# Second attention: the causal triangles move from TensorE to VectorE

## What is computed

```
q, k, v = to_heads(q), to_heads(k), to_heads(v)        # 16 heads of 16 channels
attn = jnp.einsum('bhqd,bhkd->bhqk', q, k) / math.sqrt(HEAD_DIM)
attn = attn + alibi_bias(seq_len, N_HEADS)[None] + causal_mask(seq_len)[None, None]
attn = jax.nn.softmax(attn, axis=-1)
y = jnp.einsum('bhqk,bhkd->bhqd', attn, v)
```

## Time and profile before

| | us |
|---|---|
| median of 3 runs (2758.51 to 2764.95) | 2764.04 |
| the profiled execution | 2757.35 |
| its span | 2755.6 |
| TensorE busy in the span | 2581.0 |
| VectorE busy | 1872.7 |
| ScalarE busy | 1269.7 |

### The profile page before, as it was taken

How to read it: one execution, slowest core, us unless ns; L and a number is a source line. 1 busy time by engine, 2 the same in 40 slices (tenths; PEclk the granted TensorE clock), 3 DMA queues, 4 the chain that set the end, 5 groups by cost and what they waited for, 6 DMA issues and landing times. The chain is left out here.

```text
span 2755.6 us, 38804 instructions
## 1 busy us (share of the span) xinstructions
PE 2581.0 (94%) x14106; PEld 1255.9 (46%) x14106; DVE 1872.7 (68%) x4022; ACT 1269.7 (46%) x1936; POOL 788.3 (29%) x760
## 2 busy tenths in 40 slices
PE   5987999999999999897999998899999999899998
PEld 3543333333333332354565665445544554555665
DVE  7868888788787885585664335787777776466334
ACT  4431666566566667543212322365454556321321
POOL 2545214132141300155424541311121110234441
PEclk8997999999999999899999999999999999999999
DMA  4004430331303400001303654634223440311565
GB/s 126 1 17 92 64 52 19 58 56 21 58 24 53 64 1 2 1 1 55 109 20 101 158 119 114 118 50 71 48 54 57 65 59 2 115 35 35 139 156 161
DMA packets 162592, 175.76 MB, mean 64 GB/s; under 512 B 19090, under 2 KB 135762, under 8 KB 162258
## 3 DMA queue, kind: packets, MB, share of 16 engines
q1 hardware_dynamic: 146948, 152.57, 25.4%
q0 software_dynamic: 12416, 17.84, 3.9%
q10 hardware_dynamic: 3040, 2.88, 0.4%
HBM read 116.32 MB, written 56.13 MB: 63 GB/s over the span
## 5 line engine op out<-in xcount | busy, mean ns | idle before, releaser
L1862 DVE TENSOR_REDUCE a_mx<-a_bank 128x1 f32<-128x512 f32 (+3 forms) x1792 | 1034.6, 626 | 241.7 <-PE a_bank L1595 173.1
L1730 ACT ACTIVATE a_E<-a_bank 128x1024 f32<-128x1024 f32 (+3 forms) x896 | 796.2, 931 | 401.5 <-PE a_bank L1653 273.7
L1595 PE MATMUL a_bank<-a_KT,a_QT 96*128 96x512 bf16 (+4 forms) x1792 | 572.3, 368 | 25.6 <-DVE a_mx L1862 15.2
L1653 PE MATMUL a_bank<-a_QT,a_KT 99*128 99x512 bf16 (+4 forms) x1792 | 505.1, 357 | 3.9 <-DMA a_QT<-a_mT 1.8
L1668 PE MATMUL a_bank<-a_E,a_Vg 128*32 128x512 f32 (+3 forms) x3584 | 437.3, 560 | 0.7 <-ACT a_E L1730 0.7
L1595 PEld LDWEIGHTS a_bank<-a_KT,a_QT 96*128 96x128 bf16 (+1 forms) x1792 | 152.0, 98 | 490.1 <-DVE a_mx L1862 307.5
L1653 PEld LDWEIGHTS a_bank<-a_QT,a_KT 99*128 99x128 bf16 (+1 forms) x1792 | 169.6, 98 | 173.5 <-ACT a_E L1730 31.4
L435 POOL TENSOR_TENSOR f_hl<-f_hT,f_hh 128x512 f16<-128x512 f32 x96 | 110.9, 1156 | 340.3 <-ACT f_hh L452 340.3
L903 PE MATMUL d_bank<-wdT,d_hT 128*128 128x256 f32 (+1 forms) x768 | 192.4, 393 | 4.2 <-DVE d_hT L1100 4.2
L1014 ACT ACTIVATE d_silu<-d_bank 128x512 f32<-128x512 f32 x96 | 57.1, 595 | 270.0 <-PE d_bank L888 270.0
L903 PEld LDWEIGHTS d_bank<-wdT,d_hT 128*128 128x128 f32 (+1 forms) x768 | 140.2, 191 | 63.2 <-issue 43.6
(11 more groups left out here) (235 smaller groups left out, 3633.9 us busy)
## 6 DMA issues: line engine op xcount, KB each, us to landing
parts<-a_parts SPq DMA_DIRECT2D x64, 384.0 KB, 2.6
a_QT<-parts SPq DMA_DIRECT2D x180, 128.0 KB, 5.9
a_KT<-parts SPq DMA_DIRECT2D x180, 128.0 KB, 9.1
d_wgu<-in_L_ffn_w_gate SPq DMA_DIRECT2D x64, 176.0 KB
d_wgu<-in_L_ffn_w_up SPq DMA_DIRECT2D x64, 176.0 KB
d_wd<-in_L_ffn_w_down SPq DMA_DIRECT2D x64, 176.0 KB
normalised<-d_xn SPq DMA_DIRECT2D x8, 1152.0 KB, 4.7
acc<-d_zero SPq DMA_DIRECT2D x2, 4224.0 KB, 16.4
```

The lines of the kernel that those rows point to most:

```text
L1595: last = nc.tensor.matmul(out[:, 0:w], QT[0:W, h, qt * P:(qt + 1) * P], KT[0:W, h, kh * HALF:kh * HALF + w], start=True, stop=not diag)
L1653: last = nc.tensor.matmul(out, KT[:, h, kt * P:(kt + 1) * P], QT[:, h, half * HALF + c0:(half + 1) * HALF], start=True, stop=not diag)
L1730: nc.scalar.activation(E[:, u % 2, 2 * pair:2 * pair + 2, c0:HALF], bank[:, 2 * pair:2 * pair + 2, c0:HALF], ACT.Exp).then_inc(exps, 1)
L1862: nc.vector.tensor_reduce(mx[:, x[1] // C % 2, j, qt, kh:kh + 1], out[:, 0:w], AX.X, ALU.max).then_inc(freed_dve, 1)
```

## The change

Both triangles leave TensorE. In the first pass VectorE takes the maximum of a diagonal chunk with `tensor_tensor_reduce`, which adds the tile `causal` (zeros, and the triangle in its last 128 columns) to the scores, writes the sum back and gives the maximum. In the second pass a new function `seal` has VectorE add the triangle `later` in place to the first 128 columns of both heads of a pair, one `tensor_tensor` per pair; ScalarE waits for it on a new semaphore `sealed`. The statistics tile `bnr` moves into `yT`. The core of the diff:

```diff
--- before.py
+++ after.py
@@ -40,6 +40,7 @@
 ZERO_POINT = 128.0
 LN_EPS, RMS_EPS = 1e-5, 1e-6
 NEG = -1e30
+LOWEST = -3.0e38
 VW = 32
 ROPE = HD // 2
 LIFT = 1024.0
@@ -1305,6 +1306,7 @@
     units = [(h, kt, max(0, kt - KPH * h) * P if second else 0)
              for h in range(QH) for kt in range(KPH * (h + 1) if second else TPB)]
     U = len(units)
+    diagonal = [u for u in range(U) if second and units[u][1] >= KPH * units[u][0]]
 
     chunks = [(j, qt, kh, min(HALF, (qt + 1) * P - kh * HALF) if second else HALF)
               for h in range(QH) for j in range(GH) for qt in range(h * KPH, (h + 1) * KPH) for kh in range(2)
@@ -1406,8 +1408,9 @@
         bn8 = sb(tag + "bn8", [P, TPB, 6])
         known = TPB if second else NT
         if second:
-            masks = sb(tag + "masks", [P, 2, P], BF16)
-            bnr = sb(tag + "bnr", [P, NT - TPB, 6])
+            causal = sb(tag + "causal", [P, HALF], BF16)
+            later = sb(tag + "later", [P, P], BF16)
+            bnr = yT.rearrange("p a k c -> p (a k c)")[:, 0:(NT - TPB) * 6].rearrange("p (t s) -> p t s", s=6)
         else:
             turns = sb(tag + "turns", [P, 2, T])
         bank = ps(tag + "bank", [P, 8, HALF])
@@ -1417,7 +1420,7 @@
         (root, scales, ones, normed, filled, freed_dve, freed_act, high, rest, mid, split_s, parted, parted_dve, rows_in, v_group, m_step, m_rows, scored, exps, pv, y_kept, y_step, stats,
          aggregated) = (sem(tag + n) for n in names.split())
         if second:
-            masked = sem(tag + "masked")
+            masked, sealed = sem(tag + "masked"), sem(tag + "sealed")
         else:
             t_in, shuffled, roped, roped_dve = (sem(tag + n) for n in ("t_in", "shuffled", "roped", "roped_dve"))
         if second:
@@ -1586,16 +1589,12 @@
                         b, h = G // NG, G % NG * GH + j
                         if x[1] == 0 and second:
                             pe.wait_ge(rows_in, START + 32)
-                            pe.wait_ge(masked, START + 1)
                         if x[1] % C == 0:
                             pe.wait_ge(loaded[G % NG], START + ((b + 1) * 12 + (6 if G % NG == 0 else 0)) * 16)
                         if G == 0 and qt == KPH and j == kh == 0:
                             pe.wait_ge(loaded_last, START + 6 * 16)
-                        diag = second and qt * P < kh * HALF + w <= (qt + 1) * P
                         last = nc.tensor.matmul(out[:, 0:w], QT[0:W, h, qt * P:(qt + 1) * P], KT[0:W, h, kh * HALF:kh * HALF + w],
-                                                start=True, stop=not diag)
-                        if diag:
-                            last = nc.tensor.matmul(out[:, w - P:w], ident_b[:], masks[:, 0, :], start=False, stop=True)
+                                                start=True, stop=True)
                     elif kind == "turn_m":
                         pe.wait_ge(m_step, START + (x[1] + 1) * 5)
                         last = nc.tensor.transpose(out[0:GH * 3 * TPB].bitcast(BF16)[:, 0:P],
@@ -1649,11 +1648,8 @@
                     for j in (2 * pair, 2 * pair + 1):
                         h = G % NG * GH + j
                         out = bank[:, j, c0:HALF]
-                        diag = second and kt >= KPH * half
                         last = nc.tensor.matmul(out, KT[:, h, kt * P:(kt + 1) * P],
-                                                QT[:, h, half * HALF + c0:(half + 1) * HALF], start=True, stop=not diag)
-                        if diag:
-                            last = nc.tensor.matmul(out[:, 0:P], ident_b[:], masks[:, 1, :], start=False, stop=True)
+                                                QT[:, h, half * HALF + c0:(half + 1) * HALF], start=True, stop=True)
                     last.then_inc(scored, 1)
 
                 def pv_unit(G, u):
@@ -1727,6 +1723,8 @@
                     if G == 0 and u == 1 and pair == 0 and not second:
                         act.wait_ge(roped, START + 8)
                     act.wait_ge(scored, START + G * 2 * U + 2 * u + pair + 1)
+                    if u in diagonal:
+                        act.wait_ge(sealed, START + 2 * (G * len(diagonal) + diagonal.index(u)) + pair + 1)
                     nc.scalar.activation(E[:, u % 2, 2 * pair:2 * pair + 2, c0:HALF], bank[:, 2 * pair:2 * pair + 2, c0:HALF],
                                          ACT.Exp).then_inc(exps, 1)
 
@@ -1859,7 +1857,12 @@
                     dve.wait_ge(filled, START + place[x] + 1)
                     if kind == "chunk":
                         j, qt, kh, w = chunks[x[1] % C]
-                        nc.vector.tensor_reduce(mx[:, x[1] // C % 2, j, qt, kh:kh + 1], out[:, 0:w], AX.X, ALU.max).then_inc(freed_dve, 1)
+                        dst = mx[:, x[1] // C % 2, j, qt, kh:kh + 1]
+                        if second and qt * P < kh * HALF + w <= (qt + 1) * P:
+                            nc.vector.tensor_tensor_reduce(out=out[:, 0:w], in0=out[:, 0:w], in1=causal[:, HALF - w:HALF], scale=1.0,
+                                                           scalar=LOWEST, op0=ALU.add, op1=ALU.max, accum_out=dst).then_inc(freed_dve, 1)
+                        else:
+                            nc.vector.tensor_reduce(dst, out[:, 0:w], AX.X, ALU.max).then_inc(freed_dve, 1)
                     elif kind == "turn_m":
                         dve.wait_ge(m_rows, START + x[1] * GH * 16)
                         nc.vector.tensor_copy(mT[:], out[0:GH * 3 * TPB].bitcast(BF16)[:, 0:P]).then_inc(freed_dve, 1)
@@ -1885,6 +1888,13 @@
                             statistics(b, 3)
                             aggregate(b)
 
+                def seal(G, u, pair):
+
+                    c0 = units[u][2]
+                    dve.wait_ge(scored, START + G * 2 * U + 2 * u + pair + 1)
+                    block_ = bank[:, 2 * pair:2 * pair + 2, c0:c0 + P]
+                    nc.vector.tensor_tensor(block_, block_, spread(later[:], 1, 2), ALU.add).then_inc(sealed, 1)
+
                 def statistics(b, n):
                     dve.wait_ge(freed_dve, freed_at(("out", b, n)))
                     for i in range(2):
@@ -1901,8 +1911,10 @@
                     normalise(0, i)
                 if second:
                     nc.vector.memset(mx[:], NEG)
-                    nc.vector.tensor_copy(masks[:, 0, :], core.const("mask_qk"))
-                    nc.vector.tensor_copy(masks[:, 1, :], core.const("mask_kq")).then_inc(masked, 1)
+                    nc.vector.memset(causal[:, 0:HALF - P], 0.0).then_inc(masked, 1)
+                    nc.vector.tensor_copy(causal[:, HALF - P:HALF], core.const("mask_qk")).then_inc(masked, 1)
+                    nc.vector.tensor_copy(later[:], core.const("mask_kq")).then_inc(masked, 1)
+                    dve.wait_ge(masked, START + 3)
                 else:
                     dve.wait_ge(t_in, START + 16)
                 for n in range(4):
@@ -1954,7 +1966,11 @@
                         if g == 0 and u < 4 and 0 < b < B - 1:
                             normalise(b + 1, 2 * u)
                             normalise(b + 1, 2 * u + 1)
-                        for x in beside[G, u]:
+                        for n, x in enumerate(beside[G, u] + [None] * max(0, 2 - len(beside[G, u]))):
+                            if u in diagonal and n < 2:
+                                seal(G, u, n)
+                            if x is None:
+                                continue
                             take(x)
                             if step < 4 and x[0] not in by_act:
                                 step += 1
```

## The result

The changed kernel takes 2789.18 us in the median of 4 runs (2787.30 to 2796.55), against 2761.28 us for the kernel before in 4 runs (2755.56 to 2764.95). The ratio is 1.0117, with an interval of 1.0093 to 1.0142: slower, by about 32 us (1.17% of 2761), which is small but clear of the noise. The two medians alone differ by 28 us; I go by the ratio throughout. A later set of runs of the changed kernel gave 1.0115 (1.0096 to 1.0134) and 2790.14 us.

A forecast was written before the change was run, and what follows sets the result against it. TensorE, busy 94%, was taken to bound the kernel, with VectorE nearly full in plain groups. Terms summed to -3 us, from 2757.35 to 2754 profiled, so 2761 in the median; range 2732 to 2802.

The forecast's parts named there:

- TensorE's 40 triangles give 2.3 us ... -1.5 each, -15: Ten long stretches (units 4 to 11) with projections or output: 2.3 us relief, partly used up, leaves -1.5 each, -15.
- bites only where TensorE sets the time: Second pass, exponentials waiting for the seal: fits their idle time on average, overruns by 0.2 us at worst.
- rival 1: Buffers carry VectorE's shortage across units, so TensorE's totals count: faster, 2725 to 2748, say 2737 us; chance 0.28.
- rival 2: First-pass diagonal chunks have a dear second instruction: over 8 us slower from 0.12 us each, 2799 at 0.20; chance 0.23.
- Seal 0.36 us: Second pass: each of 256 seals takes 0.36 us of VectorE, 92 us together (87 to 108).
- Diagonal chunk +0.09 us: First pass: a second instruction adds 0.09 us of VectorE per diagonal chunk, 46 us for 512; bounds 0.01 and 0.20.
- Plain groups +6.5: Five groups without projections: VectorE sets the time, 33.2 us against 31.6 if it never rests; +1.3 each taken, +6.5 together.
- Short stretches: Units 0 to 3: two with next-sequence tokens +2.4, last sequence +1, four with a projection +0.8, two with two value projections -2.
- Last group -0.5: The last group has no chunks, so its seals have room on VectorE: -0.5 us.
- Opening and first stretch +3.5: Opening with some 50 diagonal chunks, half of 4.5 us shows, +2; first short stretch of all +1.5.
- Rival 3: Late exponentials behind the seal cost each of 128 diagonal units 0.25 us: +32, 2790 us; chance 0.11.
- Rival 4: TensorE's granted clock falls to 0.90 in 16 short stretches, costing up to 14 us; chance 0.02.

The follow-up runs named there:

- the chain alone: Changed kernel with no triangle in either pass; seals add zeros to one column per bank, exponentials still wait for them: 0.9990 of the kernel before, 2756.03 us.
- the load alone: Changed kernel with no triangle taking effect; at each seal's place a 256-column SBUF maximum that nothing waits for: 1.0033 of the kernel before, 2769.24 us.
- the chunks-only kernel: Changed kernel with the second pass's triangles back on TensorE and no seals, first-pass chunks in the new form: 0.9970 of the kernel before, 2749.95 us.
- without seals: Changed kernel with no second-pass triangle or wait for one, first-pass triangle filled with zeros, chunks in the new form: 0.9897 of the kernel before, 2728.69 us.

## Why the prediction was wrong

The forecast was -3 us, the measured change +32. The measured 2789 us lies inside the stated 2732 to 2802, but only because that range takes in the slower rivals; what the forecast itself said, no change to speak of, did not happen. **The step that failed** is "TensorE's 40 triangles give 2.3 us ... -1.5 each, -15" in the ten long stretches with projections or output. They grew by 14.4 us instead, from 0.58 (the two of 23.24 us) to 2.7 (the two of 37.30). That is 29 us away from the -15, most of the miss of 35. The rest of the units came to +10.5 where I had +8.2, but term by term it is 0.2 to 2.8 us off, in both directions.

In these ten stretches taking the triangles away gives 14.2 us, not the 23 that I started from; the new form of the chunks takes 0.9; and the seals take 27.7, where I had left 8 for everything that works against the gain. Of the 27.7 the chain alone shows 14.8 and the load alone 11.1 (with up to 1.7 and 3.4 of drops of the clock in them).

What the runs put in its place:

- *The relief is worth two thirds.* The price of a triangle, 0.058 us, came from TensorE's own timeline, which is right as long as nothing else holds it. 1024 of them give 38 us, not 59: with three banks between the engines a faster TensorE waits for VectorE more often (222 waits of the chunks for 111.3 us, against 156 for 88.3).
- *The load costs also where VectorE looks idle.* 256 maxima that no other engine waits for cost 37 us. Most of it falls in the short stretches, where VectorE is full; but 11.1 fall in the ten long ones, where I had counted VectorE's 6 to 14 idle us as room. A way in which this can happen, argued and not shown: the idle time lies between its bank takings, and a seal delays the chunk behind it and with it TensorE's next one.
- *The chain costs some 19 to 26 us.* In the prediction the seal "bites only where TensorE sets the time", by 0.2 us at worst. But the longest wait of the exponentials for a seal is 3.3 us. And the prediction left out the other direction: VectorE waits at the seal for the scores, 38.2 us in all and 3.7 at the longest.
- *The clock* gives part of this. TensorE's granted clock is full in every stretch of the units before; in the changed kernel it is at half (1.2 GHz) for 13.7 us of them, in four pieces, which is at most 7 us of work. The windows around one of them:

```profile
1950.00:1963.30 13.30, 10.38 (x65) 5.15 (x63) 10.90 (x45) 4.63 (x7) 0.00 (x0) 1.00 0.10 32
1963.30:1966.70 3.40, 3.27 (x5) 1.42 (x6) 1.62 (x8) 0.50 (x1) 0.00 (x0) 0.50 0.02 5
1966.70:1980.00 13.30, 12.28 (x77) 4.33 (x75) 11.61 (x34) 6.72 (x11) 3.53 (x4) 1.00 0.09 30
```

TensorE's timeline just there (start, length, and in brackets the idle time ahead and its releaser):

```profile
1960.92 0.45 PE L1596 MATMUL a_bank<-a_KT,a_QT 102*128 102x256 bf16 x2
1963.43 0.61 PE L1596 MATMUL a_bank<-a_KT,a_QT 102*128 102x512 bf16 x1 [2.06 <-DVE a_mx L1862]
```

TensorE had idled 2.06 us for a bank; in the kernel before the same place had 1.37 us and no drop. Three of the four drops stand at such a place, the fourth in the last group. This is no rule: in the runs with seals in units 8 to 11 alone and with additions in SBUF the same three places have 2.06 us too, and only one of three is followed by a drop. What a drop costs can be read in the chunks-only kernel, where one of two equal stretches has one:

```profile
1907.32:1945.97 38.65, 35.41 (x212) 18.21 (x213) 24.56 (x85) 16.82 (x24) 6.83 (x8) 0.96 0.27 41
...
2068.26:2105.24 36.98, 33.73 (x212) 17.67 (x213) 24.56 (x85) 16.83 (x24) 6.83 (x8) 1.00 0.27 45
```

That is 1.67 us. The Trainium skill ("TensorE: Matmul & The Clock Gate", section "A second HAM failure mode: psum-queue depth-cycling") describes a TensorE whose clock swings because it idles briefly between groups as it cycles through banks. The trace agrees in so far as three of the four drops here stand beside such an idle time.

In ratios to the kernel before, measured one by one: without seals -28 us (the relief of 38, less the new chunks: 3 us by the traces, 10 by the ratios), the load +37, the chain +26 (with the small seals' own 7 in it). That sums to +35, against +32 measured. The total agrees, but by place the parts do not add up in the short stretches (the table above), so the split into load and chain is an estimate; the drops of the clock are within it.

Three sums of the prediction are also off by themselves: with the lower price of a seal (0.34) a plain group comes to 32.8 us and not 32.6, rival 1's terms give -23 and not -24, and rival 2's at 0.12 us give +7.5 and not over 8. None changes the forecast.

Point by point, by the prediction's steps:

- **Seal 0.36 us**: right, 0.33 to 0.37.
- **Diagonal chunk +0.09 us**: too dear, 0.01 to 0.05. Rival 2, a dear chunk, falls.
- **Plain groups +6.5**: +6.3, 32.92 against 31.58 us for one, and that is partly luck. I had VectorE never resting for 33.2 us, 12.2 of them in the short stretch. It is busy 31.19 us, since the chunks were cheaper, and rests 1.7 in between; the short stretch takes 10.43, and the long one 22.49 where I had 21.0. TensorE is busy 92%, not 85.
- **Short stretches**: tokens +1.7 (forecast +2.4), last sequence +0.6 (+1), the four of 12.1 us -1.0 (+0.8), the two of 13.96 us +0.6 (-2): TensorE doesn't get its time back even there.
- **Last group -0.5**: +2.3. It has hardly any chunks and so room for seals, but TensorE idles behind the chain (7.83 of 8.88 us) and its clock drops (0.81).
- **Opening and first stretch +3.5**: +3.7, of which part may be the clock.
- **Rival 1** (buffers even it out, 2737): falls. **Rival 3** (the chain, +32, 2790) hit the time, but only part of its mechanism: the chain is 19 to 26 us in all, and about half of what the seals cost in the ten long stretches; the rest is load. **Rival 4** had the wrong place: the plain short stretches stay at 1.00, and the clock drops in the stretches of 37 us.

## What to carry to other kernels

Two engines that hand each other a few banks don't share a bound that busy shares can be read against: taking 59 us from the full one gave 38, and giving 92 us to one that was busy for 70% of these stretches cost 37, most of it where it was full and some where it was not. Before moving work that a third engine waits for, run two kernels: one with the load alone at its place in the queue, and one with the waits alone on an instruction of one column; and compare them stretch by stretch, since a total can agree while its parts don't. Work that is folded into an instruction which runs anyway (here the triangle in the maximum, under 0.05 us) is the part worth keeping; a new instruction between producer and consumer was not, here.

## What the runs showed of the hardware

- The instruction that reads VectorE's accumulator has a record of 0.14 us but starts together with the instruction behind it. The whole chunk is 0.01 us dearer from start to start than a built-in maximum. What comes right behind it can be longer: another chunk of its form with 512 columns takes 0.65 us in place of 0.61, a seal 0.37 in place of 0.33, while a built-in maximum of 512 columns stays at 0.60 (trace of the changed kernel).
- An addition of 256 columns with both inputs in SBUF took 417 ns in the median and up to 1345, a maximum with one input never over 422. The Trainium skill ("SBUF — State Buffer", section "SBUF: two separate sides") says that VectorE instructions with two SBUF inputs and GpSimd instructions that read SBUF lock each other out; the trace fits it: all 21 additions of over 0.5 us overlap a GpSimd instruction that reads SBUF (its casts, copies and additions), and 216 of the other 235 overlap none. The seals of the changed kernel read one input from a bank.
- In the changed kernel TensorE's clock fell to half beside each of its three idle times of 2.06 us, in a phase in which it had been full before; with 1.37 us at the same places it never fell. One drop cost 1.67 us (read in the chunks-only kernel).
